# An adaLN block with a linear recurrence on one Trainium2 core: LN1 from chunk 4 on works on a transposed copy of x, and the output is summed by an adding transfer

## The reference, cut to what matters

```python
sa, ca, ga, sb, cb, gb = modulation rows of (silu(c) @ wmod)
h = layernorm(x) * (1 + ca) + sa                 # LN1
# attn(h): per token omega, zeta (64 values each) and F (128 values) from h,
# A = omega^2, S = 1/(1 + DT^2 A), d = 1 - zeta; a linear recurrence over time:
#   z' = d (S z - DT A S y) + F_z ;  y' = d (DT S z + S y) + F_y
# result: states @ C.T + h @ D_mat.T
x = x + ga * attn(h)
h = layernorm(x) * (1 + cb) + sb                 # LN2
xr, xk = mu_r * h + (1 - mu_r) * h_prev, mu_k * h + (1 - mu_k) * h_prev
out = x + gb * (sigmoid(xr @ W_r.T) * (relu(xk @ W_k.T)**2 @ W_v.T))
```

## Time and profile before

| | us |
|---|---|
| median of 3 runs | 980.42 (979.67 to 982.46) |
| the profiled execution | 980.24 |
| its span | 978.4 |
| PE busy in the span | 937.1 (96%) |
| DVE, ACT, POOL busy | 817.8 (84%), 696.8 (71%), 91.4 (9%) |

### The profile page before, as it was taken

The page is one execution under the profiler, slowest core; times in us unless marked ns, Lnnn a source line. Parts: engine busy times, 40 slices in busy tenths (PEclk is TensorE's granted clock), DMA queues, the critical chain, the costliest instruction groups (busy, mean ns, idle before and its releaser), DMA issues.

```text
span 978.4 us, 14767 instructions
## 1 busy us (share of the span) xinstructions
PE 937.1 (96%) x5019; PEld 786.4 (80%) x5020; DVE 817.8 (84%) x2270; ACT 696.8 (71%) x1371; POOL 91.4 (9%) x117
## 2 busy tenths in 40 slices
PE   9977968899999999999999999999999999998997
PEld 3566857788888888888888888888888888887886
DVE  4878759798898979898997989898997988697562
ACT  4979776778868686877768676886768677765451
POOL 0001001000200101110110201110020101000000
PEclk9999988899999999999999999999999999999999
DMA  9820302021221311021131302021131301111001
GB/s 328 279 76 1 108 3 84 1 88 42 72 70 44 99 44 65 23 86 44 44 97 44 97 22 88 21 87 44 44 97 44 97 7 38 44 44 44 22 22 44
DMA packets 35275, 64.78 MB, mean 66 GB/s; under 512 B 3704, under 2 KB 4344, under 8 KB 35200
## 3 DMA queue, kind: packets, MB, share of 16 engines
q1 hardware_dynamic: 35200, 63.84, 19.5%
HBM read 47.02 MB, written 16.81 MB: 65 GB/s over the span
## 4 chain that ended last, share of the span: by engine, by line
PE 84%; ACT 7%; DVE 6%; issue 1%; DMA 1%; SPq 0%; POOL 0%; DVEq 0%; ACTq 0%; POOLq 0%
PE ps_kr L328 32%; PE ps_cd L328 20%; PE ps_tv L328 18%; PE ps_pt L328 7%; PE ps_pt L336 3%; PE ps_tv L369 2%; ACT mix_full L725 1%; PE ps_tv L389 1%; ACT square_out L584 1%; DVE mix_full L977 1%; DMA x<-in_wmod 1%; PE ps_kr L389 1%; DVE tmp L1198 1%; ACT x_in L602 1%; ACT x_in L574 1%
## 5 line engine op out<-in xcount | busy, mean ns | idle before, releaser
L977 DVE SCALAR_TENSOR_TENSOR mix_full<-ps_tv,cur_m,mix_full 128x256 f32<-128x256 f32 x256 | 119.0, 479 | 42.3 <-ACT mix_full L725 42.2
L747 ACT ACTIVATE kk<-ps_kr 128x512 f32<-128x512 f32 x64 | 38.2, 598 | 124.7 <-PE ps_kr L328 124.4
L725 ACT ACTIVATE mix_full<-ps_tv,cur_m 128x255 f32<-128x255 f32 x256 | 120.1, 573 | 6.3 <-PE ps_tv L369 6.3
L1468 POOL TENSOR_SCALAR var<-sq 128x2 f32<-128x2 f32 (+1 forms) x35 | 34.4, 982 | 680.7 <-ACT square_out L584 680.7
L328 PE MATMUL ps_kr<-mix_k_hi,wk_hi 128*128 128x256 f32 x512 | 80.7, 280 | 5.6 <-issue 5.5
L328 PE MATMUL ps_kr<-mix_k_lo,wk_hi 128*128 128x256 f32 x512 | 80.0, 279 | 0.0
L328 PE MATMUL ps_kr<-mix_k_hi,wk_lo 128*128 128x256 f32 x512 | 79.7, 278 | 0.0
L328 PEld LDWEIGHTS ps_kr<-mix_k_hi,wk_hi 128*128 128x128 f32 x512 | 70.9, 190 | 8.9 <-issue 6.5
L328 PE MATMUL ps_tv<-wv_hi,kk_hi 128*128 128x512 f32 x256 | 72.0, 404 | 1.2 <-issue 1.2
L328 PE MATMUL ps_kr<-wr_hi,mix_r_hi 128*128 128x512 f32 x256 | 70.6, 398 | 2.1 <-ACT kk L747 2.1
L328 PE MATMUL ps_tv<-wv_lo,kk_hi 128*128 128x512 f32 x256 | 69.7, 394 | 0.0
(11 more groups left out here) (215 smaller groups left out, 2246.5 us busy)
## 6 DMA issues: line engine op xcount, KB each, us to landing
x<-in_x SPq DMA_DIRECT2D x32, 512.0 KB, 3.7
out<-x SPq DMA_DIRECT2D x32, 512.0 KB, 2.8
x_in<-in_x SPq DMA_DIRECT2D x15, 1024.0 KB, 5.2
x<-in_wmod SPq DMA_DIRECT2D x3, 1024.0 KB, 7.7
mix_full<-in_wmod SPq DMA_DIRECT2D x2, 1024.0 KB, 9.0
x_in<-in_x SPq DMA_DIRECT2D x2, 512.0 KB, 5.7
stage_out<-in_wd SPq DMA_DIRECT2D x1, 1024.0 KB, 10.0
stage_mix<-in_wmod SPq DMA_DIRECT2D x1, 1024.0 KB, 10.5
```

The lines of the kernel that those rows point to most:

```text
L725: mm = act.activation(mix[n][:, k, 1:UNIT], ps_tv[:, j, c * UNIT:(c + 1) * UNIT - 1], ACT.Identity, bias=cur_m[:, SHIFT + k:SHIFT + k + 1] ...
L747: act.activation(kk[:, i, :], ps_kr[:, i, :], ACT.Relu).then_inc(s_relu, 1)
L977: dve.scalar_tensor_tensor(mix[n][:, k, :], ps_tv[:, j, c * UNIT:(c + 1) * UNIT], cur_m[:, alpha + k:alpha + k + 1], mix[n][:, k, :], ALU. ...
L1468: pool.tensor_scalar(var[:, :], sq[:, :], 1.0 / D, EPS, ALU.mult, ALU.add).then_inc(s_var, 1)
```

## The change

- **LN1 path, chunks 4 to 15** (`WIDE = 4`). The host also passes x transposed (`in_xt`). SP writes rstd and -mean of the chunk to DRAM (`ln_out`), reads rstd back as a row spread over all partitions (`ln_in`, `ln_wide`), and loads the transposed chunk into `h_full` (`xt_in`, 1 MB, once the last `h_lo` of the chunk before is written). POOL issues two transfers that add the row of -mean into `h_full` (`centred`, 512 KB each). DVE multiplies by `ln_wide` (`normalised`, 2 instructions of 128x1024). `h_blocks` reads `h_full` instead of PSUM. The 16 transposes and `normalise1` of such a chunk are gone.
- **Statistics.** For these chunks ACT sums (even units, in the place of `normalise1`) and squares (odd units) chunk q + 4; `statistics1` on DVE stays for chunk 3 alone.
- **Output.** SP stores x2 as soon as the residual is added; after `read_out` POOL issues a transfer that adds `rt` (512 KB) to `out` (`add_out`). `tanh` of the next unit waits until it has landed. DVE's `add_out` is gone.
- **DVE order.** `h_low` of the second half of a chunk goes from the end of the odd unit to the start of the even one; `normalised` stands at the end of the even unit.
- **Prologue.** PE takes the first states part ahead of the projections of chunk 1, and drops 8 warming products; ACT takes the high parts of wr and wv earlier, splits `projections_out(1)`, and gives up sums and squares of chunk 3; DVE takes the low parts of wk and of h in other places.

The diff, cut to its core:

```diff
@@ SP
+            def ln_out(q):
+                sp.wait_ge(s_rstd1, q + 1)
+                sp.dma_start(ln_spread[q % 2], ln_cols[:, :, :]).then_inc(s_ln_out, 16)
+            def ln_in(q):
+                sp.wait_ge(s_ln_out, (q - WIDE + 1) * 16)
...
+                sp.dma_start(ln_wide[:, :], ln_rows[q % 2, 0:1].partition_broadcast(P)).then_inc(s_ln_wide, 16)
+            def xt_in(q):
+                sp.wait_ge(s_h_lo, q * KC)
+                sp.dma_start(h_full[:, :, :], xt_chunks[q]).then_inc(s_xt, 16)
...
-                sp.wait_ge(s_out, u * TPU + 2 * TPU)
-                sp.dma_start(out_units[u], x2[:, u % 4]).then_inc(s_stored, 16)
+                sp.wait_ge(s_x2, u * TPU + TPU)
+                sp.dma_start(out_units[u], x2[:, u % 4]).then_inc(s_stored[u % 4], 16)
...
+                    ln_out(q)
+                    if q + 1 < NCHUNK:
+                        sp.dma_start(x_in[:, :, :], x_spread[q + 1]).then_inc(s_xin, 16)
+                    ln_in(q)
+                    xt_in(q)
@@ PE
-            first_projections(1)
...
             states_part(0, ps_cd)
+            first_projections(1)
...
-            h_part(2, ps_cd, (1,))
-            keep_busy(ps_pt[:, 0, :], WARM[1])
+            pe.wait_ge(s_gated, TPU)
+            h_part(2, ps_cd)
...
-                    if q + 3 < NCHUNK:
-                        t1_first_half(q + 3)
                     r_product(u)
-                    if q + 3 < NCHUNK:
-                        rest_transposed_in(q + 3)
                 v_product(u)
@@ ACT
             def tanh(u):
-                act.wait_ge(s_out, u * TPU + TPU)
+                act.wait_ge(s_added, u * 16)
...
-            sums1(3)
-            squares1(3)
...
-                    if next_t1:
-                        normalise1(q + 3)
+                    if q + 4 < NCHUNK:
+                        sums1(q + 4)
                 else:
                     relu_squared(u)
                     if next_mix:
                         mix_high(u + 1, 0)
+                    if q + 4 < NCHUNK:
+                        squares1(q + 4)
+                    if next_cd:
+                        statistics2(u + 2)
                     if next_t1:
                         h_blocks(q + 3, (0, 1))
                         h_high(q + 3, (0, 1))
-                    if next_cd:
-                        statistics2(u + 2)
@@ DVE
+            def normalised(q):
+                dve.wait_ge(s_ln_wide, (q - WIDE + 1) * 16)
+                for j in range(2):
+                    k = slice(2 * j, 2 * j + 2)
+                    dve.wait_ge(s_centred[j], (q - WIDE + 1) * 16)
+                    dve.tensor_tensor(h_full[:, k, :], h_full[:, k, :],
+                                      ln_wide[:, :].unsqueeze(1).broadcast_to([P, 2, CHUNK]), ALU.mult)\
+                       .then_inc(s_z, 1)
...
-                        beside(rec, add_out(u - 1), 2)
-                    if next_t1:
-                        beside(rec, statistics1(q + 3), 1)
+                        if q + 2 < NCHUNK:
+                            beside(rec, h_low(q + 2, (2, 3)), 1)
+                        take(rec, 2)
...
-                    take(rec, 4)
+                    if next_t1:
+                        beside(rec, normalised(q + 3), 1)
                 else:
...
-                    beside(rec, add_out(u - 1), 2)
+                    take(rec, 4)
...
-                    if next_t1:
-                        beside(rec, h_low(q + 3, (2, 3)), 1)
             run(read_out(NUNIT - 1))
-            run(add_out(NUNIT - 1))
@@ POOL
+            def centred(q):
+                pool.wait_ge(s_xt, (q - WIDE + 1) * 16)
+                pool.wait_ge(s_ln_out, (q - WIDE + 1) * 16)
+                for j in range(2):
+                    pool.dma_start(h_full[:, 2 * j:2 * j + 2, :],
+                                   ln_rows[q % 2, 1:2].partition_broadcast(P).broadcast_to([P, 2, CHUNK]),
+                                   accum_op=ALU.add).then_inc(s_centred[j], 16)
+            def add_out(u):
+                pool.wait_ge(s_stored[u % 4], u // 4 * 16 + 16)
+                pool.wait_ge(s_rv, u * TPU + 2 * TPU)
+                pool.dma_start(out_units[u], rt[:, :, :], accum_op=ALU.add).then_inc(s_added, 16)
...
+                if u % 2 == 0 and WIDE <= q + 3 < NCHUNK:
+                    centred(q + 3)
+                if u % 2 == 1 and q + 4 < NCHUNK:
+                    rstd1_of(q + 4)
                 if u + 2 < NUNIT:
                     rstd2_of(u + 2)
+                add_out(u)
```

More of the change, by code:

```diff
@@ L169, in build @@
         s_xn1 = sem("s_xn1")
+        s_ln_out, s_ln_wide, s_xt = sem("s_ln_out"), sem("s_ln_wide"), sem("s_xt")
+        s_centred, s_z = [sem(f"s_centred{j}") for j in range(2)], sem("s_z")
         s_t1 = sem("s_t1")
@@ L588, in squares1 @@
                 act.wait_ge(s_mean1, q + 1)
-                squares(x_in, neg_mean1, square_out1, sq1, q * TPC, s_sq1)
+                if q >= WIDE:
+                    spare = x_in
+                else:
+                    act.wait_ge(s_cd, (q - 1) * TPC)
+                    spare = h[q % 2][0]
+                squares(x_in, neg_mean1, spare, sq1, s_sq1)
             def statistics2(u):
@@ L595, in statistics2 @@
                 act.wait_ge(s_mean2, u + 1)
[L596 removed]
+                squares(x2[:, u % 4], neg_mean2[:, u % 2], rt if u == 1 else xn2, sq2[:, u % 2], s_sq2)
             def normalise1(q, tiles=range(TPC)):
@@ L646, in angles_first, with omega_out @@
                 act.activation(om_exp[:, :], om_exp[:, :], ACT.Ln, bias=1.0).then_inc(s_softln, 1)
[L648 to L654 removed]
+            lower, upper = slice(0, M), slice(M, 2 * M)
+            halves = [(slice(n * M, n * M + M), slice(n * HALF, (n + 1) * HALF)) for n in range(2)]
+            def omega_out(q):
+                act.wait_ge(s_rec, (q - 1) * STEPS + STEP_RECIPROCAL)
                 act.wait_ge(s_p, q * 2 + 1)
@@ L863, in _ @@
             statistics2(3)
+            sums1(4)
+            squares1(4)
             for u in range(2, NUNIT):
@@ L1040, in read_out @@
                     dve.tensor_tensor(rt[:, i, :], ps_tv[:, i, :], rt[:, i, :], ALU.mult).then_inc(s_rv, 1)
-                    yield
-            def add_out(u):
-                for i in range(TPU):
-                    dve.wait_ge(s_rv, u * TPU + TPU + i + 1)
-                    dve.tensor_tensor(x2[:, u % 4, i, :], x2[:, u % 4, i, :], rt[:, i, :], ALU.add).then_inc(s_out, 1)
                     yield
@@ L1351, in _ @@
             beside(rec, gates(), 3)
-            weight_low("wk")
-            beside(rec, h_low(1, range(KC)), 3)
             run(rec)
-            weight_low("wr")
             for half, s_hi, s_lo in ((0, s_xs_first_hi, s_xs_first_lo), (1, s_xs_hi, s_xs_lo)):
+                run(h_low(1, (2 * half, 2 * half + 1)))
                 cols = slice(half * HALF, (half + 1) * HALF)
@@ L1360, in _ @@
             run(residual(0))
-            run(residual(1, ps_kr, rt))
-            take(later, 1)
+            run(mixer_table())
+            half_low("wk", 0)
             run(normalise2(0))
-            run(mixer_table())
-            take(later, 2)
+            half_low("wk", 1)
+            first_residual = residual(1, ps_kr, rt)
+            take(first_residual, 2)
             run(mixes(0))
             run(mix_low(0, 0))
+            run(first_residual)
+            weight_low("wr")
+            run(mix_low(0, 1))
             run(normalise2(1))
-            run(mix_low(0, 1))
-            take(later, 14)
+            take(later, 16)
             weight_low("wv")
-            take(later, 5)
+            take(later, 3)
             beside(later, mixes(1), 1)
@@ L1382, in _ @@
             run(h_low(2, (2, 3)))
-            beside(later, add_out(0), 1)
+            take(later, 2)
             beside(later, k_low(1), 2)
@@ L1386, in _ @@
             later = recurrence(2)
+            run(statistics1(3))
             run(states_low(1))
@@ L1391, in _ @@
             run(read_out(1))
+            take(later, 2)
+            run(normalise2(2))
             take(later, 8)
-            run(normalise2(2))
-            beside(later, add_out(1), 2)
+            take(later, 4)
             run(mixes(2))
```

132 lines of the change are left out of this document (81 added, 51 removed).

## The result

The changed kernel took 1010.7 us (median of 4 runs, 1009.48 to 1011.59) against 981.4 beside it: a ratio of 1.0297, with a 95% interval of 1.028 to 1.0315. It is slower by 29 us. The forecast was 978.8 with a range of 962 to 992, so the time lies 18.7 us outside.

The account below looks back on a forecast made before the run. PE was taken to bound the kernel between prologue and tail, with DVE and ACT close behind. From the profiled 980.2, -8.5 prologue, +2.4 loop and +4.5 tail gave 978.6, or 978.8 against the 980.42 median; range 962 to 992.

Parts of the forecast that it names:

- The two chains: Unit loop: the chains of DVE and ACT take PE's place at almost its own pace; chance 0.42.
- E + 14.8: Odd unit, DVE: `kk_lo` ends 14.8 us after the 8 mix transposes start; the v product waits for it, 1.5 us.
- The tail: Last chunk +2.1 us for late steps, +2.4 behind the last `read_out` (6.5 against 4.2); together +4.5.
- I take +0.2 together.: Unit loop, per chunk: +0.2 us even part, -0.1 to +0.3 odd part; +0.2 together, +2.4 over 12 chunks.
- E + 20.4: Odd unit, DVE's line: next k product starts 20.4 us after the mix transposes start, behind the v product.
- E + 20.8: Odd unit, ACT's line: `tanh`, which the next k product waits for, ends 20.8 us after the mix transposes start.
- rival C: Unit loop: chains longer than read, period 56.3 to 56.6 us, +8 to +11 for +2.4, total 984 to 988; chance 0.15.
- All of these fit, so the cost in the loop is nil.: Transfers in the loop: two adding transfers, about 5 us each, have 25 us for 1 MB; cost nil.
- Rival D: Adding transfers late, over 25 us for both or 15 for that of `out`; 5 us over gives +60, 1040; chance 0.09.
- The prologue's -8.5: Prologue: 5.0 us of PE's wait for `x_in` and about 3.5 for `xs_lo` go, earlier waits 0; -8.5 together.
- The 3.5 at `xs_lo`: Prologue, unit 2: DVE loses chunk 4's statistics and two adds; about 3.5 of PE's 3.95 us wait goes.
- Rival E: Prologue gives nothing because chunk 3's path over DVE and POOL is as late as ACT's was: 987 us; chance 0.10.

Follow-up runs that it names:

- e1: Changed kernel with one unused 32-byte tile declared ahead of `h_full`, so it and the tiles behind begin at a multiple of 64 bytes: 1010.1 us.
- e4: Changed kernel with the unused 32-byte tile ahead of `h_full` and POOL's `add_out(0)` ahead of `rstd1_of(3)`: 1000.8 us.
- e3: Changed kernel with POOL's `add_out(0)` ahead of `rstd1_of(3)` instead of behind it: 1002.3 us, ratio 1.0215.

## Why the prediction was wrong

**What held.** The two chains do take PE's place, by the mechanism that the forecast named. With PE at its old rate (e1) the steps can be read one by one: the mix transposes of the odd unit start 35.5 us behind the k product (forecast 35.3), the v product at E + 14.8 (forecast 14.8), the next k product at E + 21.1 (forecast 20.4 to 20.8). The multiplication takes 1.22 us. The tail gave +5.0 for +4.5; from the start of the last `read_out` to the end of the span it is 1008.7 - 1000.79 = 7.9 us, where it was 978.4 - 973.23 = 5.2, +2.7 for the +2.4 of the forecast. Some of this agreement is luck: the forecast's own terms there, 5 and 1, make 6.0 and not the 6.5 of its sum, the transfer took longer than 5, and the tail as a whole is +4.3 in e1 and +3.8 in e4.

**"I take +0.2 together."** This term is the step of the loop that failed. The next k product waits for the v product (E + 20.4) and for `tanh` (E + 20.8), so the later of the two decides, and the forecast's own lines give 35.3 + 20.8 = 56.1 us, +0.45 a chunk, and not +0.2. e1 shows 35.5 + 21.1 = 56.6 us in its shortest chunks, +0.95: 9 us more over 12 chunks than the forecast had. It was rival C's period, 56.3 to 56.6, to which I gave 0.15. A chain of many small terms was summed to a tenth of a microsecond and then multiplied by 12.

**The end of a sequence** is missing from the sum. The copy of `cur_m` stands behind `normalised` and ACT waits for it. Units 7, 15 and 23 take 1.4 to 1.9 us longer than their neighbours in e1, some 5 us in all. I had asked what stands behind the multiplications on DVE for the mixes only, not for this copy.

**"All of these fit, so the cost in the loop is nil."** In the loop this is true: no instruction waits for an adding transfer there. It is wrong ahead of the loop. There `add_out(0)` stands behind an instruction that waits 35 us, and 8.4 us of the 29 come from that (e3). Rival D is a late adding transfer too, but I looked for one only inside the loop, by the length of the transfer, and not at its place in POOL's queue.

**The prologue's -8.5.** With the queue repaired, unit 4 starts at 214.4 us (e4) against 215.07: -0.6, although 16 of the removed transposes stood in unit 3, ahead of it. The 5.0 at the wait for `x_in` came (7.20 to 2.0 in e3), but 2.8 went back at the next wait, and 2.4 had been lost up to unit 1, where the forecast put 0. The 3.5 at `xs_lo` didn't come: that wait is 4.95 us instead of 3.95. Rival E had this outcome, but not by its mechanism, since `x_in` of chunk 3 did come earlier. Most of the 2.4 us can be read in e4. The transposes of `x_in` of chunk 2 start at 94.62 (93.87 before), after a wait of 5.69 us (2.50 before). The v product behind them takes 103.63 - 96.24 = 7.4 us instead of 100.93 - 95.34 = 5.6. Its first two groups start 1.86 us apart and not 1.00:

```profile
96.24 2.05 PE L369 MATMUL ps_tv<-wv_hi,kk_hi 128*128 128x512 f32 x4
98.10 1.91 PE L369 MATMUL ps_tv<-wv_lo,kk_hi 128*128 128x512 f32 x4
```

The granted clock reads 0.66 from 90 to 100 us in e4 and 1.00 before. Which of the moved pieces makes the longer waits there, and the one of 7.01 us, wasn't tried, and stays open.

**The place of the tiles** is in no step. The working took every matmul at the duration of before, and for that the operands must lie where they lay. In the changed kernel this alone makes the even part 36.1 us, which PE itself needs, and hides behind it most of what the steps cost.

Of the 29.3 us the runs attribute 8.4 to the queue (e3). The rest of the loop has two causes that can't be added up, as the table shows.

## What to carry to other kernels

When an edit takes instructions away from an interleaved order, count how many steps of the interleaved chain stand ahead of the next wait before and after it: DVE's freed time went into a wait, and one number (2 for 13) was worth 28 us. When a change adds, removes or resizes any tile, compare the addresses of the matrix operands, and compare one product's duration in the two traces before anything else; a busy share of 100% hides it. An edit that gives nothing alone may be worth 15 us once another bound is gone, so a repair should be tried again after each other one.
